# Delta-rule kernel on one core: K K and K Q products by halves of the chunks, and both decay scans ahead of the solve matrices

## The reference

```
k = silu(conv(Wk h)); q, v likewise; k = k / |k|
def step(S, xs):
    kt, vt, qt, at, bt = xs
    v_old = S kt
    upd = vt - at * v_old
    S = clip(at * S + bt * (upd kt^T), -5, 5)
    ot = S qt
```

## Time and profile before

| | |
|---|---|
| median of 2 runs | 2350.57 us (2348.53 to 2352.6) |
| span of the profiled execution | 2342.8 us |
| PE busy | 1881.6 us, 80% |
| DVE busy | 1493.3 us, 64% |
| POOL busy | 991.7 us, 42% |
| ACT busy | 755.8 us, 32% |

### The profile page before, as it was taken

How to read it: one execution, slowest core, us unless ns; L and a number is a source line. 1 busy time by engine, 2 the same in 40 slices (tenths; PEclk the granted TensorE clock), 3 DMA queues, 4 the chain that set the end, 5 groups by cost and what they waited for, 6 DMA issues and landing times. The chain is left out here.

```text
span 2342.8 us, 59315 instructions
## 1 busy us (share of the span) xinstructions
PE 1881.6 (80%) x24752; PEld 1328.7 (57%) x24752; DVE 1493.3 (64%) x2188; ACT 755.8 (32%) x1250; POOL 991.7 (42%) x1315
## 2 busy tenths in 40 slices
PE   7568778789887887978878878788479984999994
PEld 4245555556555555655565555555268874666553
DVE  5446578677686777767867768675468766444332
ACT  5323333333332333333323333232134433222221
POOL 0055264461553634626536246261154420555553
PEclk9668789787786887978968879688689996999997
DMA  3302211122111221221112212111353314444442
GB/s 114 77 1 51 53 35 47 36 65 56 36 49 41 51 62 29 65 63 29 47 44 56 56 29 65 47 47 26 129 211 116 121 55 188 94 87 86 84 82 44
DMA packets 89029, 156.52 MB, mean 67 GB/s; under 512 B 15676, under 2 KB 54084, under 8 KB 87564
## 3 DMA queue, kind: packets, MB, share of 16 engines
q1 hardware_dynamic: 72860, 124.76, 17.6%
q0 software_dynamic: 15904, 27.93, 6.2%
HBM read 112.53 MB, written 40.12 MB: 65 GB/s over the span
## 5 line engine op out<-in xcount | busy, mean ns | idle before, releaser
L1100 PE MATMUL d_ps<-hT,turn_shared 128*128 128x512 f32 x768 | 428.5, 675 | 27.3 <-DMA d_cw<-convp_in 12.8
L816 DVE SCALAR_TENSOR_TENSOR turn_shared<-d_ps,d_cw,turn_shared 128x1023 f32<-128x1023 f32 (+2 forms) x288 | 365.3, 1276 | 67.0 <-ACT turn_shared L598 62.3
L757 POOL TENSOR_TENSOR d_tmp<-turn_shared 128x31 f32<-128x31 f32 (+15 forms) x496 | 281.1, 567 | 75.1 <-DVE turn_shared L920 37.5
L762 POOL TENSOR_TENSOR turn_shared<-turn_shared,d_tmp 128x31 f32<-128x31 f32 (+15 forms) x496 | 265.7, 536 | 38.9
L1100 PEld LDWEIGHTS d_ps<-hT,turn_shared 128*128 128x128 f32 x768 | 139.2, 209 | 126.2 <-issue 83.0
L637 ACT ACTIVATE d_U<-d_ps 128x128 f32<-128x128 f32 x256 | 70.2, 274 | 412.5 <-PE d_ps L1291 412.3
L598 ACT ACTIVATE turn_shared<-d_ps,d_cw 128x1024 f32<-128x1024 f32 x96 | 115.8, 1206 | 250.0 <-PE d_ps L1100 153.1
L1136 PE MATMUL d_ps<-turn_shared 64*64 64x64 f32 x4096 | 166.2, 242 | 10.8 <-ACT turn_shared L613 6.8
L2152 POOL DMA_INDIRECT out<-m_yo,m_slot_i x71 | 113.0, 1591 | 132.6 <-DVE m_yo L2252 90.7
L1136 PEld LDWEIGHTS d_ps<-turn_shared 64*64 64x64 f32 x4096 | 156.2, 157 | 16.8 <-ACT turn_shared L613 7.7
L836 DVE SCALAR_TENSOR_TENSOR d_S<-d_S,gamma_chunk,d_ps 128x64 f32<-128x64 f32 x448 | 109.0, 300 | 83.4 <-PE d_ps L1300 78.9
(11 more groups left out here) (235 smaller groups left out, 3890.6 us busy)
## 6 DMA issues: line engine op xcount, KB each, us to landing
turn_shared<-steps_scratch SPq DMA_DIRECT2D x64, 256.0 KB, 4.2
d_qg<-gamma_scratch SPq DMA_DIRECT2D x64, 256.0 KB, 4.6
y_scratch<-d_yT SPq DMA_DIRECT2D x256, 64.0 KB, 2.1
d_arow<-ab_scratch SPq DMA_DIRECT2D x128, 128.0 KB, 3.0
y<-y_scratch SPq DMA_DIRECT2D x8, 2048.0 KB, 8.3
m_w<-w_in SPq DMA_DIRECT2D x16, 512.0 KB, 10.4
turn_shared<-x_in SPq DMA_DIRECT2D x4, 1024.0 KB, 11.3
turn_shared<-x_by_half_in SPq DMA_DIRECT2D x8, 512.0 KB, 7.1
```

What stands on the lines that cost most here:

```text
L757: nc.gpsimd.tensor_tensor(tv, Tq[:, s + 1:, s].rearrange("p (r a) -> p r a", a=1).broadcast_to([P, left, known]), X[:, s, 0:known].rearran ...
L762: nc.gpsimd.tensor_tensor(X[:, s + 1:, 0:known], X[:, s + 1:, 0:known], tv, ALU.subtract).then_inc(s_sub, 1)
L816: nc.vector.scalar_tensor_tensor(out=dst[:, j + 1:], in0=src[:, 0:T - 1 - j], scalar=cw[:, u // BP % 2, n, 2 - j:3 - j], in1=dst[:, j + 1: ...
L1100: return nc.tensor.matmul(dst[:, g, :], w[:, m % 2, n, dc, :], hT[:, dc, at:at + G], start=(dc == 0), stop=(dc == DC - 1))
```

## The change

`products` takes a half of the chunks (`hf`) with both heads in place of a head with all chunks. Part `i` of a call is now four chunks with four matmuls each, in the order of `HEADS`, where it was eight chunks with two. Head h goes to the bank h of the pair of banks. The number of matmuls, their shapes and the places of the parts in the PE's order are the same. `solve_matrix` and `attention` work on the same halves. Since a half now needs the decay of both heads, `decay(u, 1)` moves from slot 2 to slot 1, ahead of `solve_matrix(u, 0)`, which now waits for both scans; and `decay(u, 0)` waits for the last product with `Dd` of the unit before.

```diff
             def decay(u, h):
                 dve.wait_ge(s_al, 32 * (2 * u + h + 1))
                 if u:
-                    dve.wait_ge(s_A, 2 * u + h - 1)
+                    dve.wait_ge(s_A, 2 * u)
...
-            def solve_matrix(u, h):
-                dve.wait_ge(s_kk, 2 * u + h + 1)
-                dve.wait_ge(s_D, 2 * u + h + 1)
+            def solve_matrix(u, hf):
+                dve.wait_ge(s_kk, 2 * u + hf + 1)
+                dve.wait_ge(s_D, 2 * u + 2)
...
-                    last = nc.vector.tensor_tensor(to[:, h * NCW:(h + 1) * NCW, :], kk[:, :, at], Dd[:, h, :, at], ALU.mult)
+                    last = nc.vector.tensor_tensor(of_half(to, hf), kk[:, :, :, at], Dd[:, :, half(hf), at], ALU.mult)
...
                     if prep and c == 1:
+                        decay(u, 1)
                         solve_matrix(u, 0)
...
                     if prep and c == 2:
-                        decay(u, 1)
                         solve_matrix(u, 1)
...
-            def products(at, other, h, i, s_done):
-                by = (lambda c, b2: kT[rows64(h), c, b2, :]) if other else (lambda c, b2: qT[rows64(h), b2, here(c)])
-                for c in range(8 * i, 8 * i + 8):
-                    for b2 in range(2):
-                        last = nc.tensor.matmul(chunks(pair(at), CW)[rows64(b2), c, :], kT[rows64(h), c, b2, :],
-                                                by(c, b2), start=True, stop=True)
+            def products(at, other, hf, i, s_done):
+                by = (lambda c, h, b2: kT[rows64(h), c, b2, :]) if other else (lambda c, h, b2: qT[rows64(h), b2, here(c)])
+                for c in range(HC * hf + 4 * i, HC * hf + 4 * i + 4):
+                    for h, b2 in HEADS:
+                        last = nc.tensor.matmul(heads_in(at)[rows64(b2), h, c % HC, :], kT[rows64(h), c, b2, :],
+                                                by(c, h, b2), start=True, stop=True)
```

More of the change, by code:

```diff
@@ L497, in half, with heads_in, of_half @@
             return slice(hf * HC, (hf + 1) * HC)
-        def of_heads(ap, hf):
-            return ap.rearrange("p (h c) -> p h c", h=2)[:, :, half(hf)].rearrange("p h c -> p c h")
+        def heads_in(at):
+            return pair(at).rearrange("p h (c t) -> p h c t", t=CW)
+        def of_half(ap, hf):
+            return ap.rearrange("p (h c) t -> p h c t", h=2)[:, :, half(hf), :]
         def u_ps(c):
@@ L893, in solve_matrix @@
                     dve.wait_ge(s_wp, 2 * u)
-                kk = chunks(pair(AT_KK[h]), CW)
+                kk = heads_in(AT_KK[hf])
                 for s, to in enumerate((TT, TTx)):
                     at = slice(s * CH, (s + 1) * CH)
-                    last = nc.vector.tensor_tensor(to[:, h * NCW:(h + 1) * NCW, :], kk[:, :, at], Dd[:, h, :, at], ALU.mult)
+                    last = nc.vector.tensor_tensor(of_half(to, hf), kk[:, :, :, at], Dd[:, :, half(hf), at], ALU.mult)
                 last.then_inc(s_tt, 1)
@@ L937, in decayed_q, with attention @@
                 nc.vector.tensor_tensor(qg[:, u % 2], qg[:, u % 2], qT[:], ALU.mult).then_inc(s_qg, 1)
-            def attention(u, h):
-                dve.wait_ge(s_kq, 2 * u + h + 1)
+            def attention(u, hf):
+                dve.wait_ge(s_kq, 2 * u + hf + 1)
                 if u >= 2:
                     dve.wait_ge(s_y, NCW * (u - 1))
-                nc.vector.tensor_tensor(A[:, u % 2, h], chunks(pair(AT_KQ[h]), CW), Dd[:, h], ALU.mult).then_inc(s_A, 1)
+                nc.vector.tensor_tensor(A[:, u % 2, :, half(hf), :], heads_in(AT_KQ[hf]), Dd[:, :, half(hf), :],
+                                        ALU.mult).then_inc(s_A, 1)
             def scale_v(u, hf):
```

## The result

The changed kernel takes 2408.33 us (median of two runs, 2405.56 and 2411.1) against 2350.57 before: the ratio is 1.025, with an interval of 1.021 to 1.028, so 58 us or 2.5% slower. The forecast was 2437 us with a range of 2392 to 2485. The profiled execution has a span of 2404.0 us, 61.2 more than before.

What follows compares the result with a forecast made beforehand. Bound: the way from the first decay scan to the end of the second solve matrix. 74 us there plus 12 us for `state(4)` make 86: span 2342.8 to 2429 us, with 7.8 us more 2437 us; range 2392 to 2485.

Steps and rivals of the forecast that it cites:

- DVE stands idle for about 3.9 us: Ahead of the moved second decay scan: DVE waits about 3.9 us for head 1's rows to land, in all iterations.
- The first solve matrices end at e + 8.5: They were to end 8.5 us after the end of an iteration's first decay scan, instead of 2.2 us.
- PE is idle until then, and then this row of work comes on the path: PE idles 5.8 us, then first Q projection, `seed_u(3)`, `state_into_u(3)` take 1.8 us at full clock, 3.1 at half.
- Half clock for the projection and the products behind it: After PE's new 5.8 us idle, the first Q projection and last K K products run at 1.2 GHz.
- The first term: Second solve matrices end later: 5.5 us in eight iterations, 3.7 in seven, 4 in iteration 0; 74 us in all.
- The term that failed: `scalars` on DVE may wait for `state(4)`: 0.8 us an iteration, 12 us in all.
- the rival with the late clock: Half clock on PE lasts through slot 4 in all iterations: 131 us more, 2482 us; chance 0.15.
- Long scans: Seven of the 32 decay scans on DVE counted as long, 3.83 us against 2.28, in iterations at half clock.
- I halve the products: Last 16 K K products on PE: 1.13 us at half clock, 0.6 at full, in place of 1.9 and 1.0.
- gain nothing: K K parts in slots 0 and 1 shrink without gain, as DVE waits for rows; K Q products lie under POOL's solve.
- The reason given for the halving: 52 ns a record on two tiles sharing their row half, taken as no gain; 27 ns with four tiles in `w_products`.
- near 280 us: Profile sign: POOL's total wait for `turn_matrix`, 210.1 us before, was to grow to near 280 us.

## Why the prediction was right, and where its sizes were off

**Right: the mechanism and the sign.** The step "DVE stands idle for about 3.9 us" measured 3.6 us by the DMA (61.1 us in 16 scans, 3.8 each). "The first solve matrices end at e + 8.5" measured e + 8.2. "PE is idle until then, and then this row of work comes on the path" measured 5.3 us of idle and 3.1 us of work ahead of the K K products (493.08 to 496.13), as said for half clock. "Half clock for the projection and the products behind it" held: the second solve matrices end at e + 13.75 to e + 14.16 in the 15 iterations, where 14.0 was said. The experiment with the rows of one head shows that the landing of the rows is the cause; that with the projection behind slot 4 shows that the projection is the carrier.

**The first term** (74 us for the later end of the second solve matrices) measured 70.6 us, the first two lines of the table. It was taken against eight iterations of before that end at e + 8.5 and seven at e + 10.3; in the trace they end at 8.3 to 11.7 with a mean of 9.4, against 9.3 by that count, so this simplification did no harm.

**The term that failed** is `state(4)`, 12 us. It is -3.9 us. I worked out how late `state(4)` would be, and set that against `scalars` as if its other release stayed where it was, though my own first term had just moved that by more than 4 us. In the kernel after both come together (502.71 and 502.95), so neither waits, and the waits that iterations of before had, as in rows 5, are gone. The clock was at 2.4 GHz again from 499 us, which leaves no slow slot 4 to pay for; the rival with the late clock (2482 us) falls with it.

**Long scans.** They were taken as seven, the same as before. They are twelve, +7.7 us: POOL's `bound_terms` and DVE's first scan start within 0.3 us of each other, and who is first decides. Why it is POOL more often in the new beat was not tried. The prediction took long scans as a mark of the iterations at half clock, and that was wrong: their length goes by POOL's step.

**The products.** "I halve the products" held for a stream at half clock: 1.08 us for 32, as said. At full clock it is 0.65 us against 0.6. That the other products "gain nothing" was too little. The stretch from the clear to the next first scan is 5.4 us shorter over the kernel. The products by heads in the same order cost 31 us more by the spans, instead of 13: 17.4 us from e to the clear, 12.9 in the wait for `state(4)`, 4.9 from the clear to the next first scan and 4.8 behind the last solve, less 7.8 for the scans (seven long in place of twelve) and 0.8 ahead of the first. The last two stretches I did not follow, and the -6.8 us behind the last solve has no cause that I tested either.

The reason given for the halving was wrong in part: rows 8 do show a gain from two quadrants that share their row half, as the last section works out, and two of them in parallel are at 52 ns and not at 27. So there was no further step to 13 ns to be had, and the halving itself came out.

**What was to be seen in the profile.** POOL's wait for `turn_matrix` "near 280 us" measured 296.9; the beat of "97 to 99 us" measured 98.65. Sum: 70.6 - 3.9 + 7.7 - 5.4 - 1.0 - 6.8 = 61.2 us, where 86 was said. The 25 us between them, and 3.5 us less between span and median (4.3 after, 7.8 before), are the distance of the forecast from the 2408 us.

## What to carry to other kernels

When a producer is delayed, list all paths that leave it up to where they meet again, and measure each against the meeting point as the other paths have moved it, not as it stood before; two paths of one length mean that shortening either buys nothing. A load into a single buffer costs its landing as soon as the two users come closer than that; the remedy here was to move both users to where their engine waits for another anyway (DVE for PE), which turned 2.5% slower into 3.0% faster. A faster stream of small products is worth what stands behind it in its queue: 63 us with nothing to cover it, 31 to 34 us with a wait beside it, from one and the same edit.

## What the runs showed of the hardware

An operation on DVE with two inputs in SBUF and one on POOL between SBUF tensors ran nearly one after the other and not at once: the scan 2.28 or 3.82 us, POOL's 128x1024 product 1.93 or 3.94, by who starts first, with 50 ns enough to turn it over. It holds for small ones too: a 128x32 product of 0.19 us took 1.47 us behind POOL's.

The rate of 64x64 f32 products goes by the number of quadrants that are used in turn. At the granted clock of 1.2 GHz a record took 52 to 61 ns with two quadrants that share their row half (96 in 5.02 us, 30 in 1.85 us), and 34 ns with all four (32 in 1.08 us), some 27 without the last one's way through. It isn't the shared row half that holds two back, nor the PSUM banks: `seed_u` uses two quadrants that share neither half and takes 0.70 us for 8 records, and `state_into_u`, which writes to the same places in PSUM from all four, takes 0.49. For the whole array, the rows at 1.2 GHz give 0.86 us for one record of 512 columns more:

```profile
757.60 2.93 PE L1100 MATMUL d_ps<-hT,turn_shared 128*128 128x512 f32 x3
```

(three records in 2.93 us in the kernel with early scans by heads, two in 2.07). Scaled to 64 columns, an estimate, that is 107 ns: two quadrants in turn halve it and four quarter it. No stream on a single quadrant was run.

In the kernel after, the clock fell to 1.2 GHz in the new idle of PE (5.2 to 6.0 us in the 15 iterations with a chain). Stretches of 1 us show it back at 2.4 GHz some 4.8 to 5.1 us after the work resumed in 14 of them (in the one shown at some 498.2, after 493.08) and 6.3 us in the first, in contrast to the 18 us or more of rows 9.
